# Laying an adjacency matrix out load by load for a graph kernel, with its first rows and first columns stored turned

## What is computed

```python
h = relu(layernorm(x))
Wh = h @ W                                   # 4096 x 128
e = leaky_relu((Wh @ a[:128])[:, None] + (Wh @ a[128:])[None, :], 0.2)
mask = (adj > 0) | eye(4096)
alpha = softmax(where(mask, e, -9e15), axis=1)
x = x + alpha @ Wh
h = relu(layernorm(x))
weights = where(dist < 1, exp(-(1/dist - 1)**2 / 0.5), 0)    # dist is adj
x = x + weights @ (h @ W1 + B1)
```

## Time and profile before

| what | value |
|---|---|
| median of the runs | 216.38 us (216.11 to 216.88) |
| profiled execution | 217.44 us |
| its span | 215.6 us |
| ACT / DVE / PE / POOL busy | 189.3 / 182.0 / 154.3 / 132.8 us |
| adjacency loads | 32, 2048 KB each, median 23.6 us from issue to landing |
| DMA packets of SyncE's queue | 18912, 71.31 MB, 84.7% of 16 engines |
| HBM read / written | 74.06 / 4.23 MB |

### The profile page before, as it was taken

One profiled execution on the slowest core, in us unless ns is written; L12 is line 12 of the kernel. 1 busy time (PEld: TensorE's weight loads), 2 busy tenths in 40 slices (PEclk: granted clock), 3 DMA queues, 4 the chain that ended last, 5 costly groups with the idle time before them and its releaser, 6 DMA issues.

```text
span 215.6 us, 3229 instructions
## 1 busy us (share of the span) xinstructions
PE 154.3 (72%) x956; PEld 103.7 (48%) x970; DVE 182.0 (84%) x535; ACT 189.3 (88%) x207; POOL 132.8 (62%) x140
## 2 busy tenths in 40 slices
PE   0186779983794992989929997499392977799472
PEld 0074565440362760549615844186341654668361
DVE  7993999999979999999488796995986499878855
ACT  0699987599899999999999999799999994999960
POOL 3980002295000588888878888888787788667450
PEclk9999999996599698599985999999979799999995
DMA  5999999999999999999999999999999999961303
GB/s 166 355 413 410 410 408 408 409 411 405 418 418 409 409 393 405 391 400 393 402 388 387 394 401 394 404 387 400 394 387 389 386 401 393 406 229 43 115 23 103
DMA packets 22259, 76.81 MB, mean 356 GB/s; under 512 B 2527, under 2 KB 3126, under 8 KB 22240
## 3 DMA queue, kind: packets, MB, share of 16 engines
q1 hardware_dynamic: 18912, 71.31, 84.7%
q0 software_dynamic: 2912, 5.22, 7.0%
q10 hardware_dynamic: 416, 0.07, 0.2%
HBM read 74.06 MB, written 4.23 MB: 363 GB/s over the span
## 4 chain that ended last, share of the span: by engine, by line
DMA 36%; DVE 31%; PE 18%; issue 7%; ACT 5%; SPq 1%; POOL 1%; POOLq 0%; DVEq 0%
DMA adj_ring<-in_adj 35%; DVE summed L1134 10%; PE bank L642 9%; DVE cand L1172 3%; ACT spread L921 3%; DVE hub_w L1415 3%; PE bank L769 2%; DVE x_sb L1458 2%; PE bank L754 2%; PE bank L761 2%; SPq L383 1%; DMA gathered_rows<-node_table,shared_index 1%; DVE stats L1114 1%; PE bank L629 1%; DVE shared_slots L1230 1%
## 5 line engine op out<-in xcount | busy, mean ns | idle before, releaser
L544 POOL DMA_INDIRECT gathered_rows<-node_table,index x48 | 76.0, 1584 | 36.5 <-DVE index L1309 22.5
L952 ACT ACTIVATE trash_a<-adj_ring,below_one 128x4096 fp8e4<-128x4096 f32 x19 | 70.4, 3705 | 5.7 <-DMA adj_ring<-in_adj 5.2
L642 PE MATMUL bank<-adj_ring,pack_w 128*128 128x512 bf16 (+3 forms) x255 | 70.0, 402 | 2.4 <-DMA adj_ring<-in_adj 1.5
L961 ACT ACTIVATE trash_a<-adj_ring 128x4096 fp8e4<-128x4096 f32 x19 | 68.7, 3614 | 0.5
L1134 DVE SCALAR_TENSOR_TENSOR summed<-adj_ring 128x4096 fp8e4<-128x4096 f32 x13 | 58.0, 4458 | 4.3 <-DMA adj_ring<-in_adj 4.2
L642 PEld LDWEIGHTS bank<-adj_ring,pack_w 128*128 128x128 bf16 x262 | 26.1, 104 | 31.5 <-issue 8.8
L544 POOL DMA_INDIRECT gathered_rows<-node_table,shared_index x24 | 33.2, 1382 | 9.6 <-issue 6.7
L1172 DVE MAX8 cand<-bank 128x8 f32<-128x120 f32 (+25 forms) x82 | 23.3, 351 | 3.9 <-PE bank L642 3.9
L769 PE MATMUL bank<-gathered_rows,spread 128*128 128x129 f32 x160 | 20.9, 282 | 3.9 <-DVE spread L1398 2.4
L769 PEld LDWEIGHTS bank<-gathered_rows,spread 128*128 128x128 f32 x160 | 19.4, 194 | 5.1 <-issue 4.8
L629 PE MATMUL bank<-codes,code_w 128*128 128x512 bf16 x25 | 11.2, 448 | 8.5 <-DMA adj_ring<-in_adj 5.6
(11 more groups left out here) (190 smaller groups left out, 258.4 us busy)
## 6 DMA issues: line engine op xcount, KB each, us to landing
adj_ring<-in_adj SPq DMA_DIRECT2D x32, 2048.0 KB, 23.6
node_table<-gathered_rows POOLq DMA_DIRECT2D x4, 520.0 KB, 8.3
x_sb<-in_x SPq DMA_DIRECT2D x8, 256.0 KB, 5.9
out<-x_sb SPq DMA_DIRECT2D x3, 512.0 KB, 14.2
gathered_rows<-node_table,index POOLq DMA_INDIRECT x48, 5.9
gathered_rows<-node_table,shared_index POOLq DMA_INDIRECT x24, 5.4
out<-x_sb SPq DMA_DIRECT2D x2, 192.0 KB, 2.1
out<-x_sb SPq DMA_DIRECT2D x1, 128.0 KB, 1.9
```

Of the source, the lines that this page charges most:

```text
L544: pool.indirect_dma_start(out=rows[:, g % RING_GROUPS * GE + t, :], out_offset=None, in_=table, in_offset=bass.IndirectOffsetOnAxis(ap=row ...
L642: last = nc.tensor.matmul(to[:, lo:hi], pack_w[:, k, :], ring_hi[:, i % AR, row_at + lo:row_at + hi], start=False, stop=(k == KB - 1), ski ...
L952: nc.scalar.activation(trash_a[:, :], ring[:, i % AR, :], ACT.Sign, bias=below_one[:, :], scale=-1.0, accum_out=signs[:, n:n + 1], saturat ...
L961: nc.scalar.activation(trash_a[:, :], ring[:, i % AR, :], ACT.Abs, accum_out=sizes[:, n:n + 1], saturate=False).then_inc(checked_a, 1)
```

## The change

The host now makes a second copy of the adjacency, `adj_laid`, in which each load lies as one contiguous block in the order in which it is read, with the diagonal set to zero; the diagonal itself is a small input of its own, `adj_own`, which VectorE checks with one short instruction. There are 33 loads instead of 32 of the same 67 MB in all: rows 0 to 127 make one load of their own, `HUB`, already turned, placed behind chunk 4; plane 0 of chunks 0, 2, 4 and 6 is left out. In the chunks of column block 0 the 128-column squares lie at the end of a partition, already turned, and the planes are 896 wide. The runs in DRAM are 8 KB (6 KB for chunks 0, 2 and 4); loads number 5 to 11, which run beside the storing of the table, keep four runs of 4 KB (3 KB for chunk 6).

`turn_hub`, `turn_columns`, `keep_hub`, `clear_diagonal` and `clean_diagonal` go. ScalarE's check of HUB (ahead of its check of chunk 5) writes `hub_mask` as the output of its second activation. Its check of chunk 8 moves to VectorE. VectorE's checks of chunks 0, 2, 4 and 6 cover three planes. `column(i)` reads the ring instead of PSUM, and a slot of column block 0 is free when `column` has run, not when the square was turned. Waits of `place` and `row_scores` for PSUM banks follow.

```diff
+HUB = CHUNKS
+LOADS = [0, 1, 2, 3, 4, HUB] + list(range(5, CHUNKS))
+BESIDE_TABLE = range(5, 12)
+def slot_of(i):
+    return LOADS.index(i) % AR
+def first_plane(i):
+    return 1 if i != HUB and chunk(i)[0] == 0 and chunk(i)[2] == 0 else 0
+def width(i):
+    return CW - P if chunk(i)[1] == 0 else CW
+def runs_of(i):
+    return HK if LOADS.index(i) in BESIDE_TABLE else 2
...
-DVE_CHECKED = [0, 1, 2, 4, 6, 10, 11, 14, 18, 20, 22, 26, 28]
-ACT_CHECKED = [i for i in range(CHUNKS) if i not in DVE_CHECKED]
-CLEARED = 6
-CLEANED = [i for i in range(CHUNKS) if is_diagonal(i) and i != CLEARED]
+DVE_CHECKED = [0, 1, 2, 4, 6, 8, 10, 11, 14, 18, 20, 22, 26, 28]
+ACT_CHECKED = [i for i in LOADS if i not in DVE_CHECKED]
...
-            def load_chunk(i):
-                s, c, h = chunk(i)
-                sp.dma_start(ring[:, i % AR, :].rearrange("p (k n) -> p k n", k=HK),
-                             adj_chunks[s, c, h]).then_inc(adj_ready[i % AR], 16)
+            def load(i):
+                lo = first_plane(i) * CW
+                laid = adj_laid[LOADS.index(i), 0:P * (HK * CW - lo)]
+                sp.dma_start(ring[:, slot_of(i), lo:HK * CW].rearrange("p (a n) -> p a n", a=runs_of(i)),
+                             laid.rearrange("(a p n) -> p a n", a=runs_of(i), p=P)).then_inc(adj_ready[slot_of(i)], 16)
...
-            for i in range(AR, CHUNKS):
-                old = i - AR
-                sp.wait_ge(packed, old + 1)
-                if chunk(old)[1] == 0:
-                    sp.wait_ge(col_turned, 2 * chunk(old)[0] + chunk(old)[2] + 1)
-                if chunk(old)[0] == 0 and chunk(old)[2] == 0:
-                    sp.wait_ge(hub_turned, old + 2)
+            for i, old in zip(LOADS[AR:], LOADS):
+                if old != HUB:
+                    sp.wait_ge(packed, old + 1)
+                    if chunk(old)[1] == 0:
+                        sp.wait_ge(col_w_set, 2 * chunk(old)[0] + chunk(old)[2] + 1)
...
-                        if i in CLEANED and 0 <= own < BW:
-                            parts = [(0, own), (own + P, BW)]
-                            nc.tensor.matmul(to[:, own:own + P], pack_w[:, k, :], clean[:, i % 2, k % HK, :],
...
+                        w = width(i) - BW if half == 0 else BW
+                        at = first * CW + (k % HK - first) * width(i) + half * (width(i) - BW)
+                        last = nc.tensor.matmul(to[:, BW - w:BW], pack_w[:, k, :], ring_hi[:, slot_of(i), at:at + w],
+                                                start=False, stop=(k == KB - 1), skip_group_check=True)
...
-                nc.scalar.activation(trash_a[:, :], ring[:, i % AR, :], ACT.Abs,
+                nc.scalar.activation(hub_mask_row if i == HUB else trash_a[:, :], ring[:, slot_of(i), :], ACT.Abs,
                                      accum_out=sizes[:, n:n + 1], saturate=False).then_inc(checked_a, 1)
...
+                if LOADS[LOADS.index(i) - 1] == HUB:
+                    check(HUB)
                 if i in ACT_CHECKED:
                     check(i)
-                if chunk(i)[0] == 0 and i % 2 == 0:
-                    keep_hub(i)
...
+                data = ring[:, slot_of(i), first_plane(i) * CW:HK * CW]
+                nc.vector.scalar_tensor_tensor(trash_v[:, first_plane(i) * CW:HK * CW], data, 1.0, data,
...
+            def check_own():
+                dve.wait_ge(own_loaded, 16)
+                nc.vector.scalar_tensor_tensor(own_trash[:, :], own_adj[:, :], 1.0, own_adj[:, :], ALU.is_ge,
...
-                dve.wait_ge(hub_kept, 2 * (next(i for i in range(0, 2 * CC, 2) if chunk(i)[1] == n // 2) // 2) + n % 2 + 1)
+                if m == 0:
+                    dve.wait_ge(checked_a, ACT_CHECKED.index(HUB) + 1)
...
-                dve.wait_ge(col_turned, 2 * s + h + 1)
+                dve.wait_ge(adj_ready[slot_of(i)], landed(i))
...
-                nc.vector.scalar_tensor_tensor(half[:, :, first:HK, :], r_half[:, :, first:HK, :], hub_whe[:, AQ:AQ + 1],
-                                               turned[:, :, first:HK, :], ALU.max, ALU.mult).then_inc(col_w_set, 1)
+                nc.vector.scalar_tensor_tensor(weights[:, :, lo:hi], r_rows[:, :, lo:hi], hub_whe[:, AQ:AQ + 1],
+                                               squares_of(i), ALU.max, ALU.mult).then_inc(col_w_set, 1)
```

More of the change, by code:

```diff
@@ L61, in chunk, with landed @@
     return s, (first + i % (2 * CC) // 2) % CC, i % 2
-def is_diagonal(i):
-    s, c, _ = chunk(i)
-    return s == c
+HUB = CHUNKS
[3 more added lines that the diff above has]
+    return LOADS.index(i) % AR
+def landed(i):
+    return 16 * (LOADS.index(i) // AR + 1)
+def first_plane(i):
[4 more added lines that the diff above has]
+    return HK if LOADS.index(i) in BESIDE_TABLE else 2
 def column_step(s):
@@ L937, in copy_projection @@
                                          ACT.Copy).then_inc(whe_copied, 1)
-            def keep_hub(i):
-                c = chunk(i)[1]
-                for half in range(2):
-                    act.wait_ge(hub_turned, i + half + 1)
-                    nc.scalar.activation(hub_mask[:, KB * c + 4 * half:KB * c + 4 * half + 4, :],
-                                         bank[4 + half][:, :].rearrange("p (b i) -> p b i", b=4),
-                                         ACT.Copy, saturate=False).then_inc(hub_kept, 1)
             def check(i):
                 n = ACT_CHECKED.index(i)
-                act.wait_ge(adj_ready[i % AR], (i // AR + 1) * 16)
+                act.wait_ge(adj_ready[slot_of(i)], landed(i))
                 if n >= 1:
                     act.wait_ge(checked_a, n)
-                nc.scalar.activation(trash_a[:, :], ring[:, i % AR, :], ACT.Sign, bias=below_one[:, :], scale=-1.0,
+                nc.scalar.activation(trash_a[:, :], ring[:, slot_of(i), :], ACT.Sign, bias=below_one[:, :], scale=-1.0,
                                      accum_out=signs[:, n:n + 1], saturate=False).then_inc(signed, 1)
@@ L1696, with laid_out @@
 _INS = ["x", "adj", "L0_gnn_W", "L0_gnn_a", "L1_gnn_W", "L1_gnn_B"]
+def laid_out(arrays, np):
+    adj = arrays["in_adj"]
+    apart = adj.copy()
+    np.fill_diagonal(apart, 0)
+    laid = np.zeros((len(LOADS), P * HK * CW), adj.dtype)
+    for n, i in enumerate(LOADS):
+        if i == HUB:
+            block = apart[:P].reshape(P, CC, P, KB).transpose(2, 1, 3, 0)
+        else:
+            s, c, h = chunk(i)
+            rows = slice(s * HR + h * HK * P, s * HR + (h + 1) * HK * P)
+            block = apart[rows, c * CW:(c + 1) * CW].reshape(HK, P, CW).transpose(1, 0, 2)[:, first_plane(i):]
+            if c == 0:
+                squares = block[:, :, 0:P].reshape(LANES, KB, -1, P).transpose(3, 1, 2, 0)
+                block = np.concatenate([block[:, :, P:].reshape(P, -1), squares.reshape(P, -1)], axis=1)
+        block = block.reshape(P, runs_of(i), -1).transpose(1, 0, 2).reshape(-1)
+        laid[n, 0:block.size] = block
+    return {"adj_laid": laid, "adj_own": np.ascontiguousarray(np.diagonal(adj)).reshape(P, NB)}
 def kernel(**inputs):
```

144 lines of the change are left out of this document (41 added, 103 removed).

## The result

The changed kernel takes 221.4 and 220.4 us in its comparable runs: 1.0208 of the kernel before [1.0156, 1.0261], some 4.5 us slower. The forecast was 217.3 (213.6 to 219.6). The profiled execution took 221.39 us with a span of 219.5; that of before 217.44 with 215.6, so the 3.9 us between the spans are what the traces have to explain.

What follows compares the result with a forecast made beforehand. Span was taken to follow scan(15)'s start, with POOL's never-waiting gathers feeding weigh(6): 171.7 + 3.5 + 3.5 - 1.4 + 0.2 + 0.2 = 177.7 against 176.78, 0.9 us later; 216.4 + 0.9 = 217.3 us (213.6 to 219.6).

Steps and rivals of the forecast that it cites:

- R1: Rival, chance 0.29: weigh(6) isn't late, the loads decide, and their whole 2.0 us gain shows: 214.4 us (212.6 to 215.2).
- The new waits on HUB and on `r_oct`: DVE's hub(0) waits for ACT's check of HUB until 56.8, PE's hub_group(0) for r_oct until about 65; claimed to cost nothing.
- R2: Rival, chance 0.20: 8 KB packets double the backlog ahead of gathers, weigh(6) comes 3.0 us later still: 220.3 us.
- R3: Rival, chance 0.09: packets cost by bytes alone, the gather stream recovers, the last load lands at 192.5 as before: 216.4 us.
- The first gather: Start of POOL's gather stream: check 8 on DVE ahead of pick(0) moves it 3.5 us, from 71.75 to 75.25.
- from chunk 6 on each chunk has the same bytes ahead of it: Load order: the planes left out come back as HUB, so bytes stay equal; chunk 8 was taken to land 0.3 us earlier.
- The stream: POOL's gathers up to group 6: +3.5 for check 26, -1.4 for lost cleans, +0.2 column steps, +0.2 longer packets; chance +-1.1.
- check 26 was to start near 165.5: DVE's check 26, freed of the turning, starts about 165.5 instead of 170.51 and holds group 6, +3.5 us.
- the 5.1 of slack: Ahead of weigh(6): group 6 landed at 171.7 and weigh(6) ran at 176.78, so 5.1 us of lateness could be absorbed.
- the column steps now read SBUF: Six DVE column steps read both matrices from SBUF and may hold gathers: 0.2 us, upper bound 2.4.
- From weigh(6) to scan(15): Chain from weigh(6) through add_columns(2) and PE's packs to scan(15): all come 0.9 us later together, with nothing added.
- The loads' gain: Longer DRAM runs mean fewer packets: the last load lands 2.0 us earlier, at 190.5 instead of 192.5.

Runs made afterwards that it cites:

- e1: The changed kernel with DVE's check of chunk 8 moved behind pick_shared(0), so nothing ahead of pick(0) waits for chunk 8: 221.0 us, ratio 1.0161.
- e2: The changed kernel with DVE's check of chunk 8 behind pick_shared(0), but the wait for chunk 8's landing kept ahead of column(7): 219.5 us, ratio 1.0124.
- e8: The changed kernel with chunk 8 checked by ACT again, as before the change: 217.8 us, ratio 1.0026.
- e5: The changed kernel with chunk 0 packed early by PE, amid the projections instead of behind all scores: 218.7 us, ratio 1.0066.
- e3: The changed kernel with 4 KB runs in every load, as before the change: 222.3 us, ratio 1.0232.
- e10: The changed kernel with ten matmuls whose result nobody reads in PE's wait ahead of add_columns(2): 217.9 us, ratio 1.0061.
- e13: The changed kernel with chunk 8 checked by ACT and ten unread matmuls in PE's wait ahead of add_columns(2): 216.6 us, ratio 1.0013.
- e15: The changed kernel with chunk 0 packed amid the projections and ten unread matmuls ahead of add_columns(2), check 8 still on DVE: 217.1 us, ratio 0.9996.
- e6: The changed kernel with DVE's check 26 behind epilogue(1) instead of ahead of weigh(6): 224.4 us, ratio 1.0294.
- e11: The changed kernel with chunk 8 checked by ACT and chunk 0 packed amid the projections: 216.5 us, ratio 0.9985.
- e12: The changed kernel with chunk 8 checked by ACT, chunk 0 packed amid the projections and ten unread matmuls ahead of add_columns(2): 214.6 us, ratio 0.9909.
- e14: The kernel before the change with only the ten unread matmuls ahead of add_columns(2) added: 216.9 us, ratio 0.9998.
- e4: The kernel before the change with only the check of chunk 8 moved from ACT to DVE, ahead of column(7): 218.8 us, ratio 1.0066.

## Why the prediction was wrong, step by step

**What held.** The kind of mechanism and the sign. The loads weren't the bound (R1); the gather stream started later, check 26 fell on group 6, weigh(6) waited for gathered rows, and `add_columns(2)` and the last packs came late with it. The new waits on HUB and on `r_oct` cost nothing on the path of the changed kernel, as said; the one on `r_oct` was next in line, though, and sets the start of the stream in e1, e2 and e8. R2 is refuted: 4 KB runs everywhere left the loss as it was, and the gathers land in a median of 5.9 us in both kernels (from the two pages, for those by `index`) and not in 8. R3 is refuted too, as 8 KB runs move 2.9% more.

**The first gather: 3.5 forecast, 7.76 measured.** The step that failed is "from chunk 6 on each chunk has the same bytes ahead of it", from which 0.3 us of earlier landing for chunk 8 were taken. The bytes are the same, but the time isn't. Chunks 0, 2 and 4 come without a plane, so the six slots that can be filled at once hold 11.0 MB instead of 12.6, and the seventh load can't be issued before PE has packed chunk 0, which is near 35.7 us. The 1.6 MB were 3.9 us of cover at 408 GB/s, and the forecast didn't ask whether the wait for the first free slot could do without them. Chunk 8 landed near 66.4 instead of 62.9, and check 8 began 3.5 us late instead of 0.3 early. The check's own term, 4.42 - 0.61 = 3.8, was right, and 0.5 came behind pick(0), where DVE waited 1.09 us for PE's words. The missing bytes explain 2.0 of the 3.5 us. The rest is within what the landing of chunk 8 varies by from one execution to the next (61.7 to 66.5 with the gap, see e5): for this one, bad luck.

**The stream: +3.5 - 1.4 + 0.2 + 0.2 = +2.5 forecast, +0.1 measured.** From the first gather to the end of group 6 both kernels need 95.3 us, although a seventh check fell under the stream. How long a check holds depends on when in it a gather starts: by the gathers' times beyond 1.0 us the six of before cost 22.4 us together, the seven of after 23.0, so 0.6 more where 3.5 was forecast. All shorter holds together came to 4.85 instead of 5.44, so the cleans that left were worth some 0.6 and not 1.4. The forecast called this chance and gave it +-1.1; it came out 2.4 on the lucky side. In the eight other kept traces of the changed layout with seven checks under the stream (e3, e5, e8, e10 to e13, e15) the same stretch took 96.6 to 99.0, around the forecast's 97.6. Another step was wrong without harm: check 26 was to start near 165.5, as column(26) needs its load alone. On DVE it also stands behind weigh(5), at 167.04 instead of 163.48, since DVE's row had waited 5.2 us for rows of the later stream before an earlier weigh; so the check began at 169.54, and it met group 6 only because the stream was 4.3 later than forecast as well. (The 60 gathers of the prediction count the first.) Together with the gap and the check this gives 7.8 + 0.1 = 7.9 us for group 6, less the 5.1 of slack 2.8, as measured at weigh(6). That the column steps now read SBUF cost next to nothing: of two gathers started under them, at 140.51 and 148.31, one took 0.99 and one 1.49. The Trainium skill (SBUF — State Buffer, Who interferes with whom) counts such a step among those that contend with GpSimd's reads; the rows agree in one of the two cases.

**From weigh(6) to scan(15): 0 forecast, 1.3 measured.** The forecast carried weigh(6)'s lateness one to one to the end. PE's row grew instead, since PE had waited longer: 3.58 instead of 2.02 for `add_columns(2)`, and 19.1 instead of 17.8 us from weigh(6) to scan(15). A longer wait on PE is not only a shift; what comes behind it can run at half clock. e13 and e6 show this from both sides; in e11 a wait of 3.31 us left the clock as it was, so it need not happen.

**The loads' gain.** 2.0 was forecast; the last load landed 0.6 earlier, at 191.9. The gain exists (2.9% from 80 us on, with the gap of 2.0 us to be made good first), but nothing in the changed kernel waits for the last load. Only e12, in which stream, queue and clock are mended, ends some 1.9 us (0.9%) ahead of the kernel before, which the same ten matmuls don't help (e14).

The parts don't add up to a sum of independent costs. Check 8 on ACT takes back 1.8%, the early pack 1.4%, the ten matmuls 1.5%, of 2.1% in all: each of them brings weigh(6) or what follows it back to where the next limit takes over. The single ratios have intervals of 0.2 to 1.1% on either side; the order of the smaller ones isn't settled.

## What to carry to other kernels

When a change takes bytes out of the first loads, compare the bytes in the slots that can be filled at once with the time until the first slot comes free; an equal total says nothing of a gap in between. Where a stream of gathers never waits, count what lies ahead of it and under it together: moving an instruction from the one to the other only changes the row in which its cost is seen. A wait that grows on PE should be priced twice, once as the shift and once by the rows at half clock behind it; work that nobody needs, put into that wait, was worth 0.8% between e11 and e12. And a row of one trace is one draw: where the start of a long stretch hangs on one landing, look at that landing in several traces before a difference of 4 us is given to an edit.

## What the runs showed of the hardware that was not expected

- PE's clock behind a wait: the length of the wait alone doesn't say what the row behind it costs. After 3.06 us (e3) `add_columns(2)` took 2.74, after 3.31 (e11) 2.02, after 3.54 (e4) 2.67, after 3.59 and more 3.56 to 3.78 (table above).
- The landing of a load varies by several us between executions: chunk 8, issued at 48.2, landed 13.5 us later in e2, 15.4 in e8 and 18.2 in the change, with the same loads ahead of it.
- With check 8 on ACT the ten matmuls narrow the spread of the times: e11's twelve runs lie between 214.5 and 218.1 us, the eight of e12 between 214.4 and 216.2 with seven within 0.6; e8's ten between 216.6 and 218.7, e13's twelve between 216.3 and 217.5. With the check on DVE they don't: e10's lie between 216.3 and 220.2, e15's between 214.6 and 218.2. There the start of the stream follows the landing of chunk 8: the first gather came 13.1 us behind it in the change and in e10, 12.6 in e5 and in e15. That this makes the spread is likely, not shown.
- A tensor_tensor on POOL is held like a gather: its scaling of the first rows took 5.12 us, begun under DVE's check of chunk 4, where that of the next rows, without a check, took 1.95. Before the change that check began 1.3 us later and held the second scaling instead (1.92, then 4.28). The first table store came some 3 us late by it, the last three 0.8, and all were done before the first index.
